# First cross attention of a six-layer fp32 kernel: x times (query weights times key weights)

## The reference

```python
x = x + _L0_xattn_ref(_layernorm(x, axis=-1), ctx_1024, ctx_1024, Wq, bq, Wk, bk, Wv, bv)

q = jnp.einsum('nkm,qm->nkq', query, Wq) + bq
k = jnp.einsum('nkm,qm->nkq', key, Wk) + bk
v = jnp.einsum('nkm,vm->nkv', value, Wv) + bv
scores = jnp.einsum('nqd,nkd->nqk', q, k) / jnp.sqrt(jnp.float32(M))
```

## Time and profile before

| | us |
|---|---|
| median of 3 runs | 1834.05 (1823.58 to 1836.29) |
| profiled execution | 1833.97 |
| its span, first to last instruction | 1832.2 |
| TensorE busy | 1648.9 (90%) |
| VectorE busy | 941.8 (51%) |
| ScalarE busy | 646.2 (35%) |
| GpSimd busy | 139.8 (8%) |

### The profile page before, as it was taken

The page is one execution under the profiler, slowest core; times in us unless marked ns, Lnnn a source line. Parts: engine busy times, 40 slices in busy tenths (PEclk is TensorE's granted clock), DMA queues, the critical chain, the costliest instruction groups (busy, mean ns, idle before and its releaser), DMA issues.

```text
span 1832.2 us, 37869 instructions
## 1 busy us (share of the span) xinstructions
PE 1648.9 (90%) x16852; PEld 1324.9 (72%) x16852; DVE 941.8 (51%) x1370; ACT 646.2 (35%) x1138; POOL 139.8 (8%) x144
## 2 busy tenths in 40 slices
PE   4988789999888999988999999999989888778887
PEld 3733677887666788877888888888777666666765
DVE  4331774336336465563555555555551465566765
ACT  2212053234434321123333333333325112366761
POOL 1200520001000000030000000000021000300003
PEclk9999899999889899999999999999989899999999
DMA  5198001111100111111111111111111000589884
GB/s 206 59 372 323 3 24 52 46 47 52 47 25 4 47 47 46 52 55 46 54 53 54 54 54 54 54 42 36 44 37 47 30 4 2 195 301 326 298 296 155
DMA packets 60129, 171.43 MB, mean 94 GB/s; under 512 B 6432, under 2 KB 23328, under 8 KB 49600
## 3 DMA queue, kind: packets, MB, share of 16 engines
q1 hardware_dynamic: 57408, 160.62, 25.3%
q0 software_dynamic: 2560, 8.39, 1.4%
HBM read 150.57 MB, written 18.35 MB: 92 GB/s over the span
## 4 chain that ended last, share of the span: by engine, by line
PE 72%; DVE 10%; issue 6%; ACT 5%; DMA 5%; POOL 2%; SPq 1%; POOLq 0%; DVEq 0%; ACTq 0%
PE PS L775 20%; PE PS L777 19%; PE PS L776 19%; DMA pool_area<-xs_dram 3%; PE PS L1151 2%; PE PS L1006 2%; PE PS L1120 2%; PE PS L882 1%; PE PS L903 1%; DVE Wl L1727 1%; PE PS L1153 1%; DVE bns L1662 1%; PE PS L1135 1%; ACT Wh L1290 1%; ACT SCP L1324 1%
## 5 line engine op out<-in xcount | busy, mean ns | idle before, releaser
L775 PE MATMUL PS<-T1h,Wh 128*128 128x512 f32 x512 | 208.6, 408 | 23.6 <-DVE T1l L1740 11.7
L776 PE MATMUL PS<-T1l,Wh 128*128 128x512 f32 x512 | 205.7, 402 | 0.0
L777 PE MATMUL PS<-T1h,Wl 128*128 128x512 f32 x512 | 205.6, 402 | 0.0
L1727 DVE TENSOR_TENSOR Wl<-W,Wh 128x2048 fp32r<-128x2048 f32 x58 | 132.8, 2291 | 109.8 <-ACT Wh L1290 109.8
L1290 ACT CAST Wh<-W 128x2048 fp32r<-128x2048 f32 x58 | 110.7, 1910 | 121.9 <-PE PS L777 110.9
L1600 POOL TENSOR_TENSOR rs<-ve,half 128x1 f32<-128x1 f32 (+1 forms) x64 | 46.8, 731 | 1386.3 <-DVE ve L1677 1060.3
L775 PE MATMUL PS<-CTh,Wh 128*128 128x256 f32 x512 | 148.0, 289 | 0.6 <-ACT SCP L1488 0.6
L776 PE MATMUL PS<-CTl,Wh 128*128 128x256 f32 x512 | 144.6, 282 | 0.0
L777 PE MATMUL PS<-CTh,Wl 128*128 128x256 f32 x512 | 144.5, 282 | 0.0
L775 PEld LDWEIGHTS PS<-T1h,Wh 128*128 128x128 f32 x512 | 100.5, 196 | 46.6 <-DVE T1l L1740 12.8
L2083 DVE COPY pool_area<-PS 128x512 f32<-128x512 f32 x64 | 44.3, 691 | 165.7 <-PE PS L777 165.7
(11 more groups left out here) (319 smaller groups left out, 3365.2 us busy)
## 6 DMA issues: line engine op xcount, KB each, us to landing
W<-units_dram SPq DMA_DIRECT2D x58, 1024.0 KB, 5.1
pool_area<-units_dram SPq DMA_DIRECT2D x23, 1024.0 KB, 6.5
pool_area<-ctx_t_dram SPq DMA_DIRECT2D x32, 512.0 KB, 4.0
T1f<-ctx_dram SPq DMA_DIRECT2D x25, 512.0 KB, 6.6
H<-ctx_t_dram SPq DMA_DIRECT2D x15, 516.0 KB, 7.9
T1f<-ctx_t_dram SPq DMA_DIRECT2D x12, 516.0 KB, 7.8
xs_dram<-pool_area SPq DMA_DIRECT2D x23, 256.0 KB, 2.3
pool_area<-xs_dram SPq DMA_DIRECT2D x23, 256.0 KB, 5.5
```

Of the source, the lines that this page charges most:

```text
L775: nc.tensor.matmul(out_, a[0], b[0], start=first, stop=False)
L776: nc.tensor.matmul(out_, a[0], b[1], start=False, stop=False)
L777: return nc.tensor.matmul(out_, a[1], b[0], start=False, stop=last)
L1727: nc.vector.tensor_tensor(low_w(u), raw(u), high_w(u).bitcast(F32), ALU.subtract).then_inc(w_split, 1)
```

## The change

q times k is x (Wq' Wk) context plus terms of the biases. The program now forms M = Wq' Wk once (48 matmuls, as many as the query product of one group), splits it into Mh and Ml, and multiplies the transposed x by it. The two query products and the low parts of q are gone. "crow" is x times a vector (the product of query weights and key bias), and the query bias becomes a vector that ScalarE adds when it drains qk. These two vectors and a number come from 33 plain fp32 matmuls with the raw weights as the stationary operand and one column moving (the last one four columns), in one bank ("wc"). Products of group 1 with M: two banks before "c" and two behind it; before, all four stood behind it. The loads are reordered, the first two transposed tiles are copied before the first weight split, and SyncE's wait in front of the CT buffers in T1 is now for the last qk product, since T1 is that product's operand.

Left out of the diff are the names of the new buffers, the semaphore `biases_ready` and the plan's lines for the new products.

```diff
@@ SyncE
-            for t in range(T):
+            for t in range(TG):
                 sp.dma_start(X[:, t, :], x[t]).then_inc(x_in[t], 16)
-            sp.dma_start(vec[:, :, :], vecs).then_inc(const_in, 16)
             load_unit(0)
             load_unit(1)
+            sp.dma_start(vec[:, :, :], vecs).then_inc(const_in, 16)
...
                 sp.dma_start(mk8[j * SEQ:(j + 1) * SEQ, :], mask).then_inc(const_in, 16)
+            for t in range(TG, T):
+                sp.dma_start(X[:, t, :], x[t]).then_inc(x_in[t], 16)
...
                 if i == CT_EARLY:
-                    sp.wait_ge(ready, J.ready["q", G - 1, C - 1])
+                    sp.wait_ge(ready, J.ready["qk", G - 1, C - 1])
...
             for i in range(CT_EARLY):
                 load_ct(i)
+            sp.wait_ge(ready, J.ready["wc",])
             load_unit(2)
@@ TensorE
-            for g in range(G):
-                for t in range(g * TG, g * TG + TG):
-                    transpose_tile("t1", t, xn, XNB["t1"])
-                w = wait_unit("0.wq")
-                wait(("t1", g * TG + TG - 1))
-                feature_major(("q",), w, T1, g)
-            wait(("q", G - 1, C - 1))
+            for t in range(TG):
+                transpose_tile("t1", t, xn, XNB["t1"])
+
+            pe.wait_ge(w_full[0], 16)
+            pe.wait_ge(w_full[1], 16)
+            pe.wait_ge(biases_ready, 1)
+            wait_banks(("wc",))
+            bk = banks(("wc",))
+            for m in range(C):
+                for c in range(C):
+                    nc.tensor.matmul(bk[:, m:m + 1], W[:, 0, c, m * P:(m + 1) * P], key_bias[:, c:c + 1],
+                                     start=(c == 0), stop=(c == C - 1))
+            for m in range(C):
+                for c in range(C):
+                    nc.tensor.matmul(bk[:, C + m:C + m + 1], W[:, 1, c, m * P:(m + 1) * P], v_("bq0")[:, c:c + 1],
+                                     start=(c == 0), stop=(c == C - 1))
+            nc.tensor.matmul(bk[:, 2 * C:3 * C], ones, both_biases, start=True, stop=True).then_inc(ready, 1)
+
+            wq, wk = wait_unit("0.wq"), wait_unit("0.wk")
+            for m in range(C):
+                wait_banks(("M", m))
+                for c in range(C):
+                    mm = split_product(banks(("M", m)), cut(wq, slice(None), c, slice(m * P, (m + 1) * P)),
+                                       cut(wk, slice(None), c, slice(None)), c == 0, c == C - 1)
+                mm.then_inc(ready, 1)
+            for t in range(TG, T):
+                transpose_tile("t1", t, xn, XNB["t1"])
+            wait(("M", C - 1))
+            w = Mh, Ml
+            feature_major(("qk",), w, T1, 0)
+            wait(("t1", T - 1))
             pe.wait_ge(small_split, 1)
-            per_token_rows("crow", B1, "bk0")
-            w = wait_unit("0.wk")
-            feature_major(("qk",), w, B1, 0)
+            per_token_rows("crow", T1, "bk0")
+            feature_major(("qk",), w, T1, 1, [0, 1])
             per_token("c", "crow", 1)
-            feature_major(("qk",), w, B1, 1)
+            feature_major(("qk",), w, T1, 1, [2, 3])
@@ ScalarE
+            high_transposes("t1", 0)
+            high_transposes("t1", 1)
             split_high(0)
...
+            high_transposes("t1", 2)
+            high_transposes("t1", 3)
+            split_high(1)
+            act.wait_ge(dve_drained, J.drain["wc",][1])
+            nc.scalar.copy(smh[:, :], sc[:, 0:NSPLW]).then_inc(small_high, 1)
+            for m in range(C):
+                act.wait_ge(ready, J.ready["M", m])
+                nc.scalar.copy(Mh[:, m, :], banks(("M", m))).then_inc(high, 1)
+            for t in range(TG, T):
+                high_transposes("t1", t)
+            drain_features(("qk",), QK, groups=[0], bias=qk_bias)
             next_after("0.wq")
             drain_rows("crow", 1)
...
-            drain_features(("qk",), QK)
+            drain_features(("qk",), QK, groups=[1], bias=qk_bias)
@@ VectorE
+            dve.wait_ge(const_in, 16 * 9)
+            link(nc.vector.memset(ones, 1.0))
+            nc.vector.tensor_tensor(both_biases, key_bias, v_("bq0"), ALU.mult).then_inc(biases_ready, 1)
             split_low(0)
+            split_low(1)
+            dve.wait_ge(ready, J.ready["wc",])
+            step(nc.vector.tensor_copy(key_bias, banks(("wc",))[:, 0:C]))
+            step(nc.vector.tensor_copy(qk_bias, banks(("wc",))[:, C:2 * C]))
+            fence()
+            nc.vector.reduce_sum(c_bias, banks(("wc",))[:, 2 * C:3 * C], AX_X).then_inc(dve_drained, 1)
             for t in range(TG, T):
                 start(t)
             for t in range(TG, TG + 2):
                 norm("n1", "t1", X, t)
-            dve.wait_ge(const_in, 16 * 9)
             for m in range(C):
-                low(("q", 0, m), B1, (A_, m, grp(0)), bias=v_("bq0")[:, m:m + 1])
+                low(("M", m), (Mh, Ml), (A_, m, A_))
...
-            split_low(1)
-            for m in range(C):
-                low(("q", 1, m), B1, (A_, m, grp(1)), bias=v_("bq0")[:, m:m + 1])
             next_after("0.wq")
             dve.wait_ge(ready, J.ready["c",])
...
-            nc.vector.tensor_scalar(cs, banks(("c",))[:, 0:T], isd, None, ALU.mult).then_inc(dve_drained, 1)
+            nc.vector.tensor_scalar(cs, banks(("c",))[:, 0:T], c_bias, isd, ALU.add, ALU.mult).then_inc(dve_drained, 1)
```

More of the change, by code:

```diff
@@ L177, in plan @@
             J.add(("t1", t), "dve", split=True)
-        for m in range(C):
-            J.add(("q", g, m), "dve", unit="0.wq", split=True)
+        if g == 0:
+            J.add(("wc",), "dve")
+            for m in range(C):
+                J.add(("M", m), "dve", unit="0.wq", split=True)
+    J.last["0.wk"] = J.last["0.wq"]
     def rows(name):
@@ L182, in rows @@
             J.add((name, g), "act")
+    features(("qk",), "act", None, 0)
     rows("crow")
-    features(("qk",), "act", "0.wk", 0)
-    J.add(("c",), "dve")
-    features(("qk",), "act", "0.wk", 1)
+    for m in range(C):
+        J.add(("qk", 1, m), "act")
+        if m == 1:
+            J.add(("c",), "dve")
     for t in range(T + 1):
@@ L344, in build @@
         Wl = sb("Wl", [P, NW, C, D], F32R)
+        Mh = nc.alloc_sbuf_tensor_at("Mh", [P, C, D], F32R, offset=area_at)
+        Ml = nc.alloc_sbuf_tensor_at("Ml", [P, C, D], F32R, offset=area_at + 4 * C * D)
         W6h = nc.alloc_sbuf_tensor_at("W6h", [P, NW6 - NW, C, D], F32R, offset=t1_at)
@@ L455, in build @@
         cst_in = sem("cst_in")
+        biases_ready = sem("biases_ready")
         const_in = sem("const_in")
@@ L542, in build @@
         CT_EARLY = 4
+        ones = pool_area[:, hi_area:hi_area + P]
+        both_biases = tiny[:, 15, 0:C]
+        qk_bias, c_bias = tiny[:, 12, 0:C], tiny[:, 12, C:C + 1]
         HT = T1f[:, 0:C * TOK].rearrange("p (c t) -> p c t", c=C)
@@ L558, in build @@
         sc = SCP[:, :, :].rearrange("p a b -> p (a b)")
+        key_bias = sc[:, 0:C * NSPL].rearrange("p (c n) -> p c n", c=C)[:, :, SPL["bk0"][0]]
         ctxl = sc[:, 0:C * BATCH].rearrange("p (c b) -> p c b", c=C)
@@ L1293, in next_after, with drain_features @@
                 split_high(UNIT[name] + NW)
-            def drain_features(name, dst, scale=1.0, groups=range(G)):
+            def drain_features(name, dst, scale=1.0, groups=range(G), bias=None):
                 for g in groups:
@@ L1299, in drain_features @@
                         act.wait_ge(ready, J.ready[name + (g, m)])
+                        if bias is not None:
+                            nc.scalar.activation(dst[:, m, grp(g)], banks(name + (g, m)), ACT.Identity,
+                                                 bias=bias[:, m:m + 1]).then_inc(act_drained, 1)
+                            continue
                         nc.scalar.activation(dst[:, m, grp(g)], banks(name + (g, m)), ACT.Copy, scale=scale).then_inc(act_drained, 1)
@@ L2230, in unit @@
         return w.reshape(C, P, D).transpose(1, 0, 2)
-    mats = [A["L0_xattn_Wq"].T, A["L0_xattn_Wk"], A["L0_xattn_Wv"].T, A["L0_attn_proj_w"].T]
+    mats = [A["L0_xattn_Wq"], A["L0_xattn_Wk"], A["L0_xattn_Wv"].T, A["L0_attn_proj_w"].T]
     for b in range(4):
```

## The result

| | before | after |
|---|---|---|
| median of 20 runs each, us | 1838.94 | 1826.91 |
| ratio, 95% interval | | 0.9931 (0.9912 to 0.9950) |
| profiled execution: span, us | 1832.2 | 1826.2 |

One run of the changed kernel, 2089.44 us at a granted clock of 0.736, is left out of the ratio.

The account below looks back on a forecast made before the run. The start of c was taken to set the first softmax and all behind it, on a chain 72% TensorE. First wide product +6.8, hole -3.5, idle -1.6, matmuls behind c -5.5: -3.6 us, 1834.0 to 1830.4; predicted 1830, range 1820 to 1838.

Parts of the forecast that it names:

- The flag: Opening, VectorE: signal that lets the bias products start, up at about 16.0 us, with the constants in by 15.7.
- The narrow products: TensorE, ahead of M: 66 records of bias products at the slow clock, 14.2 us, over at 30.2.
- the hole: TensorE's gap between M and the first product of x: 4.8 us instead of 8.3, ending at 48.8.
- the products of x: TensorE, 48.8 to c at 73.2: group 0 13.2 us with slow beginning, row product 5.7, half of group 1 5.5.
- first wide product +6.8, hole -3.5, matmuls behind c -5.5: Sum up to c: these terms and idle ahead of the row product -1.6 move c from 76.78 to 73.2, -3.6 us.
- The 20.55 us to the softmax: From c to the first softmax maximum: 20.55 us, set by code that the change leaves alone.
- the value product waits for no load: First value product, at 97.7: its load lands at 96.2, leaving 1.5 us of cover.
- A longer hole there adds nothing: TensorE ahead of the first value product: the clock fell there before too, so a longer gap costs nothing more.
- The clock did not rise in the narrow products: Rival, chance 0.20: clock rises within the bias products, 9.6 instead of 14.2 us; M fast; gain 11.0, time 1823.
- Transfers did not pace the attention: Rival, chance 0.12: 6.7 us of loads without cover appear at the first value product; loop +3.1 us, time 1837.
- The constants did come late: Rival, chance 0.13: constants come no earlier, flag at 18.4, c moves by 1.2 us only, time 1833.
- everything behind the stage shift as one: All code behind the first value product: moves by the same 3.6 us as c, 1834.0 to 1830.4.

Follow-up runs that it names:

- after_again: The changed kernel, unchanged, profiled a second time: c at 70.28, stage end 217.02 us; no timed ratio.
- The two runs on the loads: Kernel before with the change's load order and first copies: ratio 0.9966 to before; changed kernel with the old order of loads and first split: 0.9971.
- before_again: The kernel before, unchanged, profiled a second time: c at 75.09, stage end 221.24 us; no timed ratio.
- before_loads: Kernel before with only the change's load order and first two tile copies, both query products kept: ratio 0.9966 to the kernel before.
- narrow_late: Changed kernel with the 33 narrow matmuls moved behind the weight product, between the transposes of tiles 5 and 6: ratio 0.9928 to the kernel before.
- narrow_twice: Changed kernel with the 32 narrow matmuls for the two bias vectors done twice: ratio 1.0052 to the kernel before.
- prefetch: Changed kernel with the first three context tiles in other buffers, loaded ahead of the last product of x: ratio 0.9950 to the kernel before.
- narrow_spread: Changed kernel with setup ahead of c, contexts loaded early, narrow products spread into waits and between wide ones: 1811.57 us, ratio 0.9849 to the kernel before.
- loads_setup: Kernel before (old algebra) with the change's load order and first copies, and the setup drawn ahead of c: ratio 0.9959 to the kernel before.

## Right or wrong, step by step

**Up to c.** Predicted 73.2, measured 70.67 and 70.28. The flag came at 17.5 (16.6 in after_again), not 16.0: the constants still ended a wait at 17.01 (16.13), not by 15.7. VectorE had also lost 1.5 us before it on an x tile, but without that it would only have waited longer for the constants. The narrow products took 14.06 us (14.2). M took 12.92 (13.8) and the hole 4.08 (4.8). The large miss is the products of x: 22.1 us from 48.58 to c where I had 24.4, because the clock did not fall in the short hole and the product of group 0 had no slow beginning. I had taken it over from a hole of 8.3 us. That the opening and not the algebra would bring the gain up to c stood in no step: I had booked it as "first wide product +6.8, hole -3.5, matmuls behind c -5.5", with the earlier flag inside the first term. The two runs on the loads show it.

**From c to the end of the stage.** The 20.55 us to the softmax held (20.45), and the value product waits for no load, as forecast. "A longer hole there adds nothing" is settled only in part. Behind the hole TensorE runs slowly, for 10 us in after; windows of after:

```profile
92.00:94.00 2.00, 0.55 (x3) 0.28 (x3) 1.31 (x6) 0.52 (x2) 0.00 (x0) 0.93 1.05 407
94.00:96.00 2.00, 0.85 (x4) 0.23 (x8) 0.84 (x4) 0.97 (x4) 0.00 (x0) 0.50 1.05 393
102.00:104.00 2.00, 2.00 (x10) 0.90 (x9) 0.00 (x0) 0.00 (x0) 0.00 (x0) 0.51 0.96 369
104.00:106.00 2.00, 2.00 (x19) 1.16 (x17) 0.00 (x0) 0.00 (x0) 0.00 (x0) 1.00 1.04 419
```

In before it was some 3.5 us (0.50 at 102 to 104, 0.92 after it), and the third softmax follows c by 33.55 there and by 36.27 in after: 2.7 us lost. But before_again has the long stretch as well, without a longer hole:

```profile
100.00:102.00 2.00, 2.00 (x12) 0.81 (x9) 0.00 (x0) 0.00 (x0) 0.00 (x0) 0.50 1.04 408
106.00:108.00 2.00, 2.00 (x10) 0.75 (x10) 0.00 (x0) 0.11 (x1) 0.00 (x0) 0.50 1.03 412
```

All kernels with the setup in its old place have 33.4 to 34.1 us there (before, before_loads, narrow_late, narrow_twice) or 36.3 to 36.6 (the other six). The slow stretch lasts 3.4 to 6.8 us in the four and 10.2 to 13.7 in the six. It is a matter of two values, not of the change; what decides between them stays open. With two profiles of each, the stage ends 4.0 to 4.2 us earlier, against 3.6 predicted.

**The rivals.** The clock did not rise in the narrow products (narrow_twice). Transfers did not pace the attention (prefetch). The constants did come late, by 1.5 us of flag, but other terms (products of x -2.3, M -0.9, hole -0.7) more than paid for it.

**The rest of the time.** I let everything behind the stage shift as one. That step failed, and with it the size of the gain: the stage gives 4 us, the timed gain is 12.7. From the stage end to the first expert tile the four profiles with the old algebra take 1379.3 to 1383.2 us (mean 1381.1), the ten with the new one 1372.3 to 1381.0 (mean 1376.0), in code with no edit. The timings agree: with the new algebra the ratio gives 4 to 9 us more than the stage end moved (after: -12.7 and -4.0; narrow_spread: -27.8 and -21.1; narrow_twice alone, +9.5 and +8.5, does not fit), in before_loads and loads_setup less than 1. For after that is 8.7 us, more than the 5 that the means of the profiles show; the difference stays open. Most of the 5 us, 3.6, lies in the attention of layer 3: 92.8 to 94.2 us with the old algebra, 87.2 to 91.3 with the new. There the products of probabilities and values come in runs of 64 small matmuls, 128 records. TensorE at the third of these runs, first in the timeline and the windows of before:

```profile
553.93 0.18 PE L1020 MATMUL PS<-SCP,pool_area 32*32 32x32 f32 x1 [1.69 <-issue]
```

```profile
554.00:556.00 2.00, 2.00 (x7) 1.62 (x7) 1.63 (x4) 0.59 (x1) 0.56 (x1) 0.72 0.03 8
556.00:558.00 2.00, 2.00 (x6) 1.53 (x5) 0.00 (x0) 0.00 (x0) 0.00 (x0) 0.50 0.00 0
```

Then in those of after:

```profile
546.14 0.31 PE L1059 MATMUL PS<-SCP,pool_area 32*32 32x32 f32 x19 [0.41 <-issue]
```

```profile
548.00:550.00 2.00, 2.00 (x43) 1.52 (x42) 1.24 (x4) 0.55 (x2) 0.56 (x1) 1.00 0.00 0
550.00:552.00 2.00, 2.00 (x130) 1.80 (x103) 0.00 (x0) 1.97 (x6) 0.00 (x0) 1.00 0.03 8
```

In front of the run's last record TensorE of before stops for 1.69 us, put down to nothing ("issue"), and the clock then falls to 0.50; after stops for 0.41, 18 records earlier in the run, and keeps 1.00. The other three profiles with the old algebra stop in front of the same record as before (1.59, 1.70 and 2.46; behind the 2.46, in loads_setup, the clock stays at 1.00). None of the ten with the new algebra has a stop of more than 0.41 in this run. From the start of this run to the start of the next the four take 11.4 to 12.3 us and the ten 8.9 to 9.3, so some 2.9 of the 3.6 us lie here. The stop belongs to the program, then, and not to chance.

What TensorE waits for can be seen as well. The pages of before and after list a DMA queue of the kind "instruction" (columns: packets, MB, share of 16 engines):

```profile
q8 instruction: 134, 2.20, 0.5%
```

Its packets are 16 KB each, one for every 126 of the 16852 matmul records in before. Counted from the program's start, the stops of before and after stand in front of the same record, the 3088th: the change puts 18 records more ahead of the run (66 narrow ones for 48 wide). The last packet ahead of the stop landed at 552.52 in before and at 544.78 in after, and TensorE went on 1.41 and 1.36 us later. It is the same elsewhere. Behind 500 us the fourteen traces have 86 stops over 0.9 us put down to "issue"; but for one of 2.1 us at a fixed place in each, all of them, 72, end 1.2 to 1.6 us after such a packet landed. So these are waits for TensorE's own instructions, as far as places and times can show it, and an edit that changes their number shifts where the packets fall in all that follows. Why this packet comes later in the run with the old algebra stays open. The remaining 1.5 us of the 5 lie in stages that also scatter within one kernel (the fifth layer's took 120.26 us in before and 117.96 in before_again).

## What to carry over

Fusing two weight products pays only as far as what it adds can lie under other work: here 14 us of tiny products ate the gain of a 48-matmul product until they were spread into waits and between wide products. Before you credit an idea, run its side edits alone: load order and two copies gave all that this change gained up to c. And compare two profiles of each kernel, stage by stage, before you explain a gap that is larger than the stage you changed: adding or removing matmuls can move a stop in code that no edit touched.

## What was not expected of the hardware

The narrow fp32 products hold TensorE fully busy and yet let its granted clock fall (to 0.50 in narrow_late) and leave it at the slow pace for 28 us (narrow_twice). At either level their price is plain: 0.22 us a record slow, 0.11 to 0.12 fast.

VectorE's setup instructions take 1.19 to 1.25 us each beside GpSimd's eight additions (10.04 us, 1.255 each), one per addition, while like ones ahead of them took 0.17 to 0.24. The Trainium skill, "SBUF — State Buffer", section "SBUF: two separate sides", says that the two engines share a pair of ports, which VectorE needs for an instruction with two operands in SBUF or in a mode that uses both of its ports, and that one instruction holds the pair to its end while the other is blocked. The trace agrees, with 1.24 beside 1.255. Eight such instructions fill the 10 us from 78.81 on, and GpSimd's powers the 5.9 before; ahead of c all of it ran under the products of x.

A stop of 1.6 to 2.5 us in a far stage, at a place that no edit touched, stood in all four profiles of the old algebra and shrank to 0.41 or less in all ten of the new; in three of the four the granted clock fell to 0.50 behind it. It ended 1.4 to 1.6 us after a packet of TensorE's instructions had landed.
